# Adaptive-layernorm block (linear attention and a routed feed-forward) on one core: key weights converted as they land, tail attention behind a shared step, a routing chain over seven steps, and turned rows loaded by ScalarE in the last stage

## The reference, cut to what matters

```python
mod = (silu(c) @ wmod).reshape(4, 6, 1, 512)           # sa, ca, ga, sb, cb, gb
h = layernorm(x) * (1 + ca) + sa                        # x: 4 x 1024 x 512
q, k, v = relu(h @ Wq), relu(h @ Wk), h @ Wv            # 16 heads of 32
vk = v_pad @ k^T per head and batch (sum over 1024 rows)
o = (vk @ q)[:-1] / ((vk @ q)[-1:] + 1e-15)
x = x + ga * (o @ w_proj.T + b_proj)
h = layernorm(x) * (1 + cb) + sb
scores = sigmoid(h @ gate_w.T); top 2 of 8 experts by scores + bias
y = sum over the 2 experts of weight * (silu(h W1) * (h W3)) W2      # inner size 352
shared = (silu(h sw1) * (h sw3)) sw2                                  # inner size 704
x = x + gb * (y + shared)
```

## Time and profile before

| | us |
|---|---|
| median of 3 runs (lowest, highest) | 1355.58 (1349.45, 1356.57) |
| profiled execution, its own time | 1354.19 |
| its span, first to last instruction | 1352.4 |
| PE busy | 1234.7 (91%) |
| DVE busy | 660.1 (49%) |
| mean granted clock of PE, share of full speed | 0.968 |

### The profile page before, as it was taken

How to read it: one execution, slowest core, us unless ns; L and a number is a source line. 1 busy time by engine, 2 the same in 40 slices (tenths; PEclk the granted TensorE clock), 3 DMA queues, 4 the chain that set the end, 5 groups by cost and what they waited for, 6 DMA issues and landing times.

```text
span 1352.4 us, 25210 instructions
## 1 busy us (share of the span) xinstructions
PE 1234.7 (91%) x9054; PEld 784.3 (58%) x9054; DVE 660.1 (49%) x1382; ACT 413.1 (31%) x869; POOL 395.2 (29%) x367
## 2 busy tenths in 40 slices
PE   6998999999997889878886999999999999989998
PEld 1645565565565656545553555656656665666675
DVE  3646767877876666677764211111111111135455
ACT  2423433433443432422233122222222222212121
POOL 1212555655654433100000111111111111056552
PEclk9999999999999999988897999999999999989999
DMA  5714687897886857633344466565565556399976
GB/s 194 221 47 116 163 195 192 196 224 161 203 216 183 231 157 201 200 101 119 112 131 140 106 141 137 122 140 135 125 137 140 126 135 138 92 245 237 234 215 171
DMA packets 269204, 219.08 MB, mean 162 GB/s; under 512 B 188496, under 2 KB 200784, under 8 KB 268572
## 3 DMA queue, kind: packets, MB, share of 16 engines
q1 hardware_dynamic: 241560, 158.45, 46.4%
q0 software_dynamic: 12848, 35.40, 11.6%
q10 hardware_dynamic: 14680, 23.62, 5.6%
HBM read 116.69 MB, written 56.94 MB: 128 GB/s over the span
## 4 chain that ended last, share of the span: by engine, by line
PE 37%; DMA 9%; DVE 9%; issue 1%; ACT 1%; SPq 0%; ACTq 0%; DVEq 0%; POOLq 0%
PE ps_o L84 6%; PE ps_o L85 6%; PE ps_o L86 6%; PE ps_vs L84 5%; PE ps_vs L86 4%; PE ps_vs L85 4%; DMA xt<-g 4%; DMA out<-xc 2%; DVE tile_is L867 2%; DMA s_ht<-h2t_d 1%; DVE w_all L682 1%; PE ps_y L1393 1%; DVE s_xs L677 1%; PE ps_vh L84 1%; DMA w_stage<-in_w_d 1%
## 5 line engine op out<-in xcount | busy, mean ns | idle before, releaser
L471 POOL DMA_INDIRECT g<-h_d,slot_token x71 | 67.3, 949 | 521.7 <-DMA xt<-g 347.0
L84 PE MATMUL ps_o<-w_all,xt 128*128 x568 | 178.3, 314 | 14.3 <-DMA xt<-g 14.1
L85 PE MATMUL ps_o<-w_all,xt 128*128 x568 | 178.3, 314 | 0.0
L86 PE MATMUL ps_o<-w_all,xt 128*128 x568 | 178.2, 314 | 0.0
L913 DVE TENSOR_TENSOR at<-ps_y,at 128x384 f16<-128x384 f32 x71 | 39.6, 557 | 176.5 <-ACT at L1165 176.5
L908 DVE SCALAR_TENSOR_TENSOR a<-ps_o,a 128x352 f32<-128x352 f32 x71 | 37.2, 525 | 173.7 <-PE ps_o L86 173.7
L1170 ACT ACTIVATE y<-ps_vs,slot_weight 128x512 f32<-128x512 f32 x71 | 48.8, 688 | 230.5 <-PE ps_vs L86 230.5
L84 PE MATMUL ps_qh<-ht,wqkv 128*128 128x128 f16 x512 | 88.6, 221 | 9.6 <-DVE qt L549 7.1
L86 PE MATMUL ps_qh<-ht,wqkv 128*128 128x128 f16 x512 | 88.7, 221 | 0.0
L85 PE MATMUL ps_qh<-ht,wqkv 128*128 128x128 f16 x512 | 88.6, 221 | 0.0
L84 PE MATMUL ps_kh<-s_ht,sh 128*128 128x256 f16 x256 | 72.9, 285 | 13.2 <-DMA s_ht<-h2t_d 11.5
(11 more groups left out here) (240 smaller groups left out, 3179.8 us busy)
## 6 DMA issues: line engine op xcount, KB each, us to landing
y_d<-y SPq DMA_DIRECT2D x71, 256.0 KB, 3.4
w_stage<-in_w_d ACTq DMA_DIRECT2D x64, 176.0 KB, 2.5
xb<-in_x SPq DMA_DIRECT2D x32, 256.0 KB, 3.1
xr<-in_x SPq DMA_DIRECT2D x32, 256.0 KB, 4.0
x_d<-x SPq DMA_DIRECT2D x32, 256.0 KB, 3.0
h_d<-hl SPq DMA_DIRECT2D x32, 256.0 KB, 2.6
h2t_d<-h2t SPq DMA_DIRECT2D x32, 256.0 KB, 3.4
s_ht<-h2t_d SPq DMA_DIRECT2D x32, 256.0 KB, 3.6
```

Of the source, the lines that this page charges most:

```text
L84: nc.tensor.matmul(out, lh, rh, start=first, stop=False, skip_group_check=True)
L85: nc.tensor.matmul(out, lh, rl, start=False, stop=False, skip_group_check=True)
L86: return nc.tensor.matmul(out, ll, rh, start=False, stop=last, skip_group_check=True)
L471: pool.indirect_dma_start(m.g[:, t % 2, :], None, m.h2_d, bass.IndirectOffsetOnAxis(ap=m.slot_token[:, t:t + 1], axis=0)).then_inc(m.gathe ...
```

## The change

Six edits, in five places.

1. Start: `split_high` and `split_low` of the four key pieces move ahead of the first modulated row (ACT first waits for the last `wmod` load, then issues loads 4 and 5, then splits pieces 0 to 3). The other eight are spread: 4 and 5 around `h_high`/`h_low` of slot -2, 6 and 7 of slot -1, 8, 9 and 10, 11 of slot 0. The `wmod` loads and the copy of `mod` in slot 0 come after `v_high`.
2. Tail: PE does `up(q)` before `attend(t)`, and a due `down` after it. DVE and ACT keep their order.
3. Middle: the routing chain takes seven steps, 22 to 28 (`bias_scores`, `pick_first`, `pick_second`, `weigh`, `add_runs`, `place`, `name_slots`); masks run in steps 29 to 44 and `list_tokens` in step 46.
4. Middle: in each step DVE does `low(q - 1)` before the masks.
5. Middle: the routing tables lie in the room of the last expert alone, so 77 pieces are split by step 46 and 11 after it, in steps 47 to 49.
6. Last stage: ACT issues the `s_ht` loads, for chunk n + 1 right behind its activation of the first step of chunk n, one step earlier than SP did, and without waiting for `h2t_stored`.

```diff
+SPLITS_FIRST = {-2: (4,), -1: (6,), 0: (8, 9)}
+SPLITS_LAST = {-2: (5,), -1: (7,), 0: (10, 11)}
-TURNS_FROM = TAIL_STEPS + 5
+TURNS_FROM = TAIL_STEPS + 7
-LAST_PIECES = 3
-SHARED_PIECES = (E - 2) * WP
+LAST_PIECES = 4
+SHARED_PIECES = (E - 1) * WP
...
@@ sync_program, last stage
-        if j == 1:
-            load_h(n + 1)
@@ vector_program, slots
-        if s == -2:
+        if s == -3:
             for n in range(KC):
                 split_low(n)
...
+        for n in SPLITS_FIRST.get(s, ()):
+            split_low(n)
...
         h2_low(t - 2)
+        for n in SPLITS_LAST.get(s, ()):
+            split_low(n)
@@ vector_program, middle
-    beside = {TAIL_STEPS: (pick_first,), TAIL_STEPS + 1: (pick_second,), TAIL_STEPS + 2: (weigh,), TAIL_STEPS + 3: (add_runs,),
-              TAIL_STEPS + 4: (place,), LIST_STEP: (list_tokens,), LIST_STEP - 1: (name_tiles,)}
+    beside = {TAIL_STEPS: (bias_scores,), TAIL_STEPS + 1: (pick_first,), TAIL_STEPS + 2: (pick_second,), TAIL_STEPS + 3: (weigh,),
+              TAIL_STEPS + 4: (add_runs,), TAIL_STEPS + 5: (place,), TAIL_STEPS + 6: (name_slots,), LIST_STEP: (list_tokens,),
+              LIST_STEP - 1: (name_tiles,)}
     for q in range(TAIL_STEPS, EARLY_STEPS):
         multiply(q)
+        low(q - 1)
         for t in list_turn(q):
             masks(t)
-        low(q - 1)
@@ scalar_program
+    act.wait_ge(m.wmod_loaded[KC - 1], 16)
     for n in range(KC, STAGE_RING):
         load_stage(n)
+    for n in range(KC):
+        split_high(n)
...
+        if q % SH_TILES == 0:
+            load_h(q // SH_TILES + 1)
@@ tensor_program, slots
-        attend(t)
         if s >= TILES:
             q = STEPS_PER_SLOT * (s - TILES)
             up(q)
-            if down_due(q):
-                down(q // SH_TILES - 1)
+        attend(t)
+        if s >= TILES and down_due(q):
+            down(q // SH_TILES - 1)
```

More of the change, by code:

```diff
@@ L807, in pick_first @@
     def pick_first():
-        bias_scores()
         pick(0)
@@ L1112, in scalar_program @@
             h2_high(t - 2)
-        v_high(s)
+        for n in SPLITS_LAST.get(s, ()):
+            split_high(n)
+        if s == -2:
+            load_stage(STAGE_RING + 2)
+            load_stage(STAGE_RING + 3)
+        if s == -1:
+            load_stage(STAGE_RING + 4)
+            load_stage(STAGE_RING + 5)
+        v_high(s)
+        if s == 0:
+            act.dma_start(m.bproj[:, :], m.b_proj.partition_broadcast(B)).then_inc(m.c_loaded, 16)
+            act.dma_start(m.gstage[:, :, :], m.gate_t.rearrange("(k p) e -> p k e", p=P)).then_inc(m.c_loaded, 16)
+            for k in range(KC):
+                act.dma_start(m.wmod[:, k, 2 * C:6 * C], m.wmod_d[k * P:(k + 1) * P, 2 * C:6 * C]).then_inc(m.wmod_loaded[k], 16)
+            act.wait_ge(m.mod_done, 1)
+            act.activation(m.mod[:, 0:C], m.ps_y[0:B, :], ACT.Copy).then_inc(m.mod_copied, 1)
         o_high(t)
@@ L1178, in scalar_program, with load_h @@
     e_high(SLOT_TILES - 1)
+    def load_h(n):
+        if n < CHUNKS:
+            act.wait_ge(m.up_done, SH_TILES * (n - 1))
+            for u in range(2):
+                act.dma_start(m.s_ht[:, n % 2, u, :, :].rearrange("p j n -> p (j n)"), m.h2t_d[2 * n + u]).then_inc(m.s_ht_loaded[n % 2], 16)
     for q in range(EARLY_STEPS, SH_TILES * CHUNKS):
         activate(q)
+        if q % SH_TILES == 0:
+            load_h(q // SH_TILES + 1)
         if q == EARLY_STEPS:
```

51 lines of the change are left out of this document (18 added, 33 removed).

## The result

The changed kernel takes **1333.49 us**, median of 4 runs (1328.03 to 1337.95), for 1352.91 of the kernel before in the same session (4 runs): ratio 0.985, 95% interval 0.981 to 0.990, so 13 to 26 us less. The forecast was 1313, 1299 to 1330. The direction holds, the size does not: half of the forecast 41 us is there, and the time lies above the range.

What follows compares the result with a forecast made beforehand. PE, busy 1234.7 of 1352.4 us, was taken as the bound, its 117.7 us of idle time, apart from the clock, the most to gain. Terms -6.5 - 6.5 - 19.5 - 8.5 = -41 from 1354.2 gave 1313 us, range 1299 to 1330.

Steps and rivals of the forecast that it cites:

- Start: Start: earlier splits bring the first key matmul to 23.5 and the query to about 32.5; -6.5 us.
- Tail: Tail: `up` before the attention covers seven waits of 8.6 us in all; -6.5 us, ends -8.6 and 0.
- it fits with 1.8 to spare: Tail: the chain from attention to landed turn takes 7.1 us, within the 8.9 until `project_out`.
- `up(q + 3)` alone waits for the activation: Tail: the later `activate(q)` delays only `up(q + 3)`, three steps on; +1.1 us set for this and other effects.
- The first rival: Tail and middle: VectorE and ScalarE become the bound; tail -2, middle -12, total 1325 us; chance 18%.
- (a): Middle, steps 22 to 30: earlier `low` and later masks remove waits, partly replaced by others; -4 us.
- (b): Middle, two six-step periods: `low` ahead of the masks shortens each from 34.0 to 31.1 to 31.2; -6 us.
- (c): Middle, from step 43: fewer last pieces bring the first expert matmul 10 us earlier, the 9.04 wait shrinking to about 3.
- the last pieces at about 20 us earlier than before: Middle, steps 47 to 49: with 11 pieces left instead of 22, the last are done about 20 us earlier.
- the second rival: Middle's end: expert weights end no earlier, held by `up(49)` and a later list; middle -10, total 1323 us; chance 10%.
- Last stage: Last stage: ACT's early loads remove three `s_ht` waits, 3 to 5 us returning for `low`; -8.5 us, ends -4 and -11.
- signs of being wrong: Tail and middle: waits for `ot` in the tail, periods of 34, or a wait of 9 ahead of the first expert.

Runs made afterwards that it cites:

- c_start_back: Changed kernel with the start's weight splits in the order of before again: 1341.1 us, ratio 0.989 to the kernel before.
- b_step_first: Changed kernel with ScalarE and VectorE doing the shared step ahead of the attention's results in the tail: 1336.2 us, ratio 0.988 to the kernel before.
- b_low_back: Changed kernel with `low` behind the masks again: 1339.5 us, ratio 0.989 to the kernel before.
- a_route_back: Changed kernel with the five-step routing chain, 66 expert pieces ahead of the list and 22 behind again: 1337.4 us, ratio 0.985 to the kernel before.
- c_pieces49: Changed kernel with the four last expert pieces loaded and split ahead of step 49's own work: 1324.4 us, ratio 0.978 to the kernel before.
- d_best_route_back: Changed kernel with slot 31's row loads early, step 49's pieces first, five-step routing and 22 last pieces: 1329.6 us, ratio 0.984 to the kernel before.
- a_sht_back: Changed kernel with SyncE loading the shared expert's turned rows again, at each sixth's second step: 1341.3 us, ratio 0.989 to the kernel before.
- d_best_tail: Changed kernel, slot 31's loads early, step 49's pieces first; tail: shared step first on ScalarE and VectorE, `o_low` before `xg` on GpSimd: 1322.9 us, ratio 0.977.
- the control: The changed kernel unaltered, run again beside three part-removals: 1335.2 us, ratio 0.984 to the kernel before.
- e_olow_dve: Changed kernel, slot 31's row loads early, step 49's pieces first; VectorE instead of GpSimd makes `o_low` in the tail: 1322.7 us, ratio 0.979.
- b_pool_order: Changed kernel with GpSimd making `o_low` ahead of the same tile's `xg` addition in the tail: 1332.7 us, ratio 0.985 to the kernel before.

## Why the prediction was half right

**Start, right.** -6.5 forecast, -7.0 in the profile (3.4 to 8.1 in the profiles of all the kernels with this start), and 6 us in c_start_back. The walk of the splits on both engines held within 0.2 us at both matmuls that it named.

**Tail, wrong: the step that failed is "it fits with 1.8 to spare".** The chain of 7.1 us was added up from durations, each from its own row, and two of them were taken without the queue that they stand in. `o_low` was 1.35, but from `o_high`'s end to the turn's issue it is 2.8, behind `h` and `xg` on POOL, and the earlier trace rows had 2.85 there already (453.22 to 456.07). The turn was 3.7, the median of the turns of `ht` in the whole kernel, but it lands after 4.1, 5.7, 3.8 and 3.2 in the first four slots, and the turns of `ot` in the tail of the kernel before had a median of 4.7 over the seven issued from 436 to 530. Added from start to start, the chain in the slot shown above is 9.2 us, from the attention's end at 454.96 to a landing at 464.20, and the forecast had 8.9 to hand. And "`up(q + 3)` alone waits for the activation" left out the `down`: `activate(q)` behind `o_high` puts `low(q - 1)` behind it as well, which the next `down` needs at once, 3.97 us in slot 38. The first rival, VectorE and ScalarE become the bound, at 18%, had the moved attention only shift the wait, with -2 for the tail and -12 for the middle; +1.4 came, which is inside the tail's scatter and so no change, and -14.2. Its sum of 1325 is 3 us from the profiled execution and 8 from the median, the nearest of the named cases. That the wait only shifts is shown; that VectorE and ScalarE are what bounds the tail is not. The rule of the Trainium skill ("TensorE: Matmul & The Clock Gate", "Architectural detail: the array is 16× 32×32, not 1× 128×128") that both queues are strictly first in, first out would have made the tail 0. The number agrees, and the row of slot 38 shows the rule at work; but b_step_first, which puts both queues into the new order, doesn't get the gain back, so it is not the whole of the reason.

**Middle, two of three parts right.** (a) -4 for -4.7 and (b) -6 for -4.5. In (b) `low` alone brings 6.6 (b_low_back), and the 11 pieces more ahead of the list take 2.7 back (a_route_back). (c) failed: -10 forecast, -5.0 came. The step was "the last pieces at about 20 us earlier than before": counted from up(43), the last piece ends at 39.1 us for 47.5, 8.5 earlier. The number of pieces was walked, and not where the last ones stand, behind `activate(49)`, which waits for up(49) behind a `down`; the second rival, at 10%, had named that hold. c_pieces49 and d_best_route_back show it from both sides: with the hold gone the wait is 4.15, and only then the routing edits count. A second step of (c) failed too: it kept the 8.0 us from the last piece to the first expert matmul, and they are 11.5 now, 3.5 of the missing 5, since the turn stands behind the loads of `s_xs` on SyncE and lands later. So the wait of 9.04 became 6.75 and not 3. The recorded sum of the three parts, -20.5, is by its own terms -20; I had taken -19.5.

**Last stage, right in kind.** -8.5 forecast, -6.4 in the profile; a_sht_back gives 6 in the medians. The three waits went. "Some 3 to 5" of waiting for `low` was forecast for the first `down`, and 4.0 came there; with two later ones, which the forecast did not have, they are 6.1 in this stage for 1.1. The Trainium skill ("DMA: Bandwidth & Descriptors", "Issuing engines are not separate DMA queues") by itself would have left 8 of the gain out; a_sht_back shows that the move brought 6, and the loads' issue 7 to 8 us behind their step that the cost was their place in SyncE's order, behind stores that are waited for, which the rule doesn't speak of.

**The sum.** Tail 7.9 and (c) 5 are 13 of the 15 us by which the profile missed the forecast of -41. Another 7 lie between profiles and medians: the profiled execution of the changed kernel is the fastest of its four, and the medians differ by 19.4, not 26.1. Runs of one kernel scatter by 0.7% here, 10 us, and my range, made of terms alone, had no room for that. Of the signs of being wrong that the prediction named, the waits for `ot` in the tail came; the periods of 34 and the wait of 9 did not.

## What to carry to other kernels

A wait that disappears is worth its length only if the queues behind it have as much to spare. Add up the chain not from the durations of its operations but from start to start as the trace has them, since each operation's place behind others on its engine and the landing time of its transfer in that very stretch are part of it; three edits whose waits stood alone (a start, a `low` behind the masks, a load behind stores) gave the whole gain, one inside a loop over five engines gave nothing, and one whose gain another engine's queue held gave nothing until that hold was gone. Then look, for each late result, at what stands ahead of it in its engine's queue without need: two such changes of order, a few lines each, brought another 17 us.

## What was not expected of the hardware

VectorE's `low` takes 0.41 us alone and up to 1.49 when it starts behind one of GpSimd's instructions, `h2_low` 0.69 and up to 1.64. Where VectorE starts first it keeps its time: in the kernel before, `low` at 454.61 took 0.41 though `o_low` started at 454.69, and in d_best_tail `h2_low` takes 0.744 on average over ten (1.335 in the control), though in seven of them GpSimd's next addition begins while it runs. From up(0) to up(22) the means were 1.19 for `h2_low` and 0.63 for `low` in the kernel before, and are 1.34 and 0.73 in the control: a move of matmuls by 2.7 us changed the durations of instructions that it didn't touch, by changing which of the two engines starts first.

Turns of the same size landed between 3.2 and 7.4 us after their issue within one tail (e_olow_dve). In the changed kernel the slow one, 5.7 us, was issued amid the first loads of the shared expert's rows; in the kernel before, two later ones, issued at 505.09 and 514.82, took 4.8 and 4.7 as well. Issuing a turn 0.8 us earlier (b_pool_order) did not land it earlier.
